# Two hundred and eight groups of softmax work in an engine loop of eight pairs a turn, with four logit banks and two message banks

## The chip, the cores and the metric

The kernel runs on one core of a Trainium2 chip. The metric is the device time of one execution in microseconds, as the median of the runs shown. The engines of the core are TensorE (PE; its weight loads are listed apart, as PEld), VectorE (DVE), ScalarE (ACT), GpSimd (POOL) and SyncE (SP), which here only starts transfers.

## The reference

Four graph layers run one after the other over a graph of 3125 nodes with 16 features and 100,000 edges sorted by destination. The change is in the second layer, a softmax over the incoming edges of each node, for each of 16 x 16 channels:

```python
w_m = (efeat @ W_msg + b_msg).reshape(E, in_f, -1)
w_a = (efeat @ W_attn + b_attn).reshape(E, in_f, -1)
h_src = feat[src][:, :, None]
e1 = w_m * h_src
e2 = w_a * h_src
seg_max = jax.ops.segment_max(e2, dst, num_segments=N)
ex = jnp.exp(e2 - seg_max[dst])
denom = jax.ops.segment_sum(ex, dst, num_segments=N)
attn = ex / denom[dst]
ft = jax.ops.segment_sum(e1 * attn, dst, num_segments=N)
return ft.sum(axis=1)
```

Around it stand a gated layer (`L0`), four graph convolutions (`L2`) and a sheaf layer (`L3`), each behind a layer norm and added to `x`.

## The kernel before

The program is a row of stages, each with its own stream of instructions per engine and a barrier behind it. The first stages sort the edges by blocks of 128 destination nodes (`NB` = 25 blocks) into 832 tiles (`NT`) of 128 slots, 416 pairs of tiles that never straddle two blocks, and 208 groups (`HT`) of four tiles (`HB`). Then come the middle stage (names `mid_`, written out on all engines), the update of the gated layer, the segment maximum (`segment_max`, names `mx_`, an engine loop on all engines, with gathers of node rows by GpSimd, L1236), `split_top` (the maxima as three bf16 parts, `m.top3`), and the stage that is changed, `soft_sums` (names `sm_`). Behind it come `attend`, a bucket table and the adjacency, the convolutions, the sheaf stage (names `sh_`, again a loop with gathers) and the end.

`soft_sums` is written out in full, with no loop on any engine. For a pair `r` of tiles:

- TensorE, `network(r)`: two bf16 matmuls into the logit bank `net_a` (L1564) and two into the message bank `net_m` (L1565), from the loaded edge features and the weights; one signal, `net_s`. There are three banks of each (`sets`), and the function waits for `both_s`, so for `weigh` of pair `r - 3`.
- VectorE, `enter(r)`: multiplies both by the features of the source nodes (`m.held`), L1506 (`arg_s`) and L1507 (`mess_s`).
- TensorE, `top(r)`: six bf16 matmuls (L1578) take the block's maxima from the logits, spread by the one-hot `hot_t`; `tops_s`.
- ScalarE: the exponential, L1549, into the first half of `both`; `exp_s`.
- VectorE, `weigh(r)`: messages times exponentials, L1512, into the second half; `both_s`.
- TensorE, `spread(r)`: two fp32 matmuls (L1591, recorded as four, with four weight loads) sum `both` over the slots of each node by the one-hot `hot`; `sums_s`.
- VectorE, `add(r)`: L1523, adds that to the block's part of `m.acc`; `kept`.

VectorE also makes the one-hots of each group, `hot_t` (L1495) and `hot` (L1223), and clears `m.acc` first (L1525). The order of the work is written out by hand. In step `r` TensorE does `network(r+3)`, `top(r+2)`, `spread(r+1)`, and VectorE `far_hot`, `enter(r+2)`, `weigh(r+1)`, `add(r)`, `spread_hot`. The block numbers are read into registers for eight pairs at a time (`blocks_of`). SP loads for each group the destination row (`low`, L1471) and the features (`feat`, L1472) into two halves, when `net_s` and `hot_t_s` say that the older ones are used.

GpSimd does other work meanwhile: once `rec2` and `row2` are loaded (L1474, L1475, behind the first two groups' loads on SP's queue), it scatters the records of the 832 tiles into a second order in DRAM (`slots2`), by 832 written-out indirect transfers (L1481) with no wait between them, and waits for all of them at the end.

Of the kernel before, what the change touches and what calls it, by code (L numbers as in the profile page):

```python
# [5 lines left out]
ALU = mybir.AluOpType  # L6
# [3 lines left out]
I32 = mybir.dt.int32  # L10
BF16 = mybir.dt.bfloat16
# [1431 lines left out]

def soft_sums(nc, m):

    turns, sets = NT // 2, 3
    with ExitStack() as ctx:
# [5 lines left out]
        net_a, net_m = ([ps(f"{n}{k}", [P, 2, 256]) for k in range(sets)] for n in ("net_a", "net_m"))  # L1453
        sums = [ps(f"sums{k}", [P, 512]) for k in range(2)]
        loaded = [sem("loaded0"), sem("loaded1")]
        names = ("hot_t_s", "hot_s", "net_s", "arg_s", "mess_s", "tops_s", "exp_s", "both_s", "sums_s", "kept", "cleared",
                 "ordered", "order_in")
        (hot_t_s, hot_s, net_s, arg_s, mess_s, tops_s, exp_s, both_s, sums_s, kept, cleared, ordered,
# [3 lines left out]
        @block.sync  # L1462
        def _(sp):
            low_rows = m.low_row.rearrange("(c n) -> c n", n=512)
            feats = m.feat_t.rearrange("k (c n) -> k c n", n=512)
            for n in range(HT):
                h = n % 2
                if n >= 2:
                    sp.wait_ge(net_s, 2 * n - 2)
                    sp.wait_ge(hot_t_s, n - 1)  # L1470
                sp.dma_start(low[:, h], low_rows[n:n + 1].to_broadcast([P, 512])).then_inc(loaded[h], 16)  # L1471
                sp.dma_start(feat[:, h], feats[:, n, :]).then_inc(loaded[h], 16)  # L1472
                if n == 1:
                    sp.dma_start(rec2[:, :, :], m.rec2_dram).then_inc(order_in, 16)  # L1474
                    sp.dma_start(row2[:, :], m.row2_dram).then_inc(order_in, 16)  # L1475
# [13 lines left out]
        def _(dve):  # L1489
            def far_hot(n):  # L1490
                h = n % 2
                dve.wait_ge(loaded[h], (n // 2 + 1) * 32)
                if n >= 2:
                    dve.wait_ge(tops_s, 2 * n - 2)
                nc.vector.tensor_scalar(hot_t[:, h], low[:, h], m.iota_col[:, 0:1], None, ALU.is_equal).then_inc(hot_t_s, 1)  # L1495

            def spread_hot(n):
                if n >= 2:
                    dve.wait_ge(sums_s, 2 * n - 2)
                one_hot(nc, m, LO, n, hot[:, n % 2]).then_inc(hot_s, 1)  # L1500

            def enter(r):
                k = r % sets
                src = m.held[:, 2 * r:2 * r + 2, :][:, :, :, None].to_broadcast([P, 2, D, D])
                dve.wait_ge(net_s, r + 1)
                nc.vector.tensor_tensor(four(net_a[k][:, :, :]), four(net_a[k][:, :, :]), src, ALU.mult).then_inc(arg_s, 1)  # L1506
                nc.vector.tensor_tensor(four(net_m[k][:, :, :]), four(net_m[k][:, :, :]), src, ALU.mult).then_inc(mess_s, 1)  # L1507

            def weigh(r):
                dve.wait_ge(exp_s, r + 1)  # L1510
                dve.wait_ge(mess_s, r + 1)
                nc.vector.tensor_tensor(both[:, r % 2, :, 1, :], net_m[r % sets][:, :, :], both[:, r % 2, :, 0, :], ALU.mult).then_inc(both_s, 1)  # L1512

            values = []

            def add(r):
                if r % 8 == 0:
                    values[:] = blocks_of(nc, m, mybir.EngineType.DVE, r, 8)
                row = m.acc[:, bass.ds(values[r % 8], 1), :].rearrange("q o c -> q (o c)")
                dve.wait_ge(sums_s, r + 1)  # L1520
                if r:
                    dve.wait_ge(kept, r)
                nc.vector.tensor_tensor(row, row, sums[r % 2][:, :], ALU.add).then_inc(kept, 1)  # L1523
# [715 lines left out]
```

## Time and profile before

| | us |
|---|---|
| runs | 10386.8 and 10391.05 |
| median | 10388.92 |
| profiled execution, span | 10386.0 |
| TensorE busy | 6161.5 (59%) |
| VectorE busy | 6112.8 (59%) |
| GpSimd busy | 4395.4 (42%) |
| ScalarE busy | 1635.9 (16%) |

The span runs from the first to the last instruction of one profiled execution; no time of its own is listed for what lies around it, and it is 0.8 us below the faster of the two runs. Busy shares are means over all the stages, which have different limits, so they say little of the one stage that is changed; the profile has to be cut by stage.

### The profile page before, as it was taken

To read this page: it belongs to the slowest core of one execution; us is meant where nothing else is said; L and a number is where in the kernel's file an instruction comes from. 1 tells how busy PE (TensorE), PEld (TensorE's weight loads), DVE (VectorE), ACT (ScalarE), POOL (GpSimd) and SP (SyncE) were. 2 spreads that over 40 slices of the span, in tenths; PEclk is the share of its full clock that TensorE was granted. 3 is DMA by queue.
4 is the path that set the end of the run, shared out by engine and by line. 5 is a ranking of instruction groups with operands and counts; after the bars stand their busy time and mean duration, and the time that the engine had idled before them with its cause. 6 is when DMAs were issued, how large, how long until landed. Compare 5 with 4: busy or idle time off the path is not lost. (4 is left out here: it accounts for less than half of the span.)

```text
span 10386.0 us, 121636 instructions
## 1 busy us (share of the span) xinstructions
PE 6161.5 (59%) x33600; PEld 4039.5 (39%) x33601; DVE 6112.8 (59%) x12781; ACT 1635.9 (16%) x2872; POOL 4395.4 (42%) x4142
## 2 busy tenths in 40 slices
PE   4433333144456777761111499984469967777799
PEld 2333332034455444440000255543434345555555
DVE  6666663143346777772000399999950056666798
ACT  0111110000012444330000022213400011222100
POOL 0577775456653666656777400000000055565300
PEclk9999997555557898885555699998999955555599
DMA  2222223111112222230000011112235611111000
GB/s 79 46 54 52 52 53 78 32 43 32 34 40 58 64 66 66 62 62 12 4 4 5 16 43 43 43 34 76 105 156 230 253 24 25 25 25 25 15 0 1
DMA packets 491139, 554.08 MB, mean 53 GB/s; under 512 B 259701, under 2 KB 390093, under 8 KB 477394
## 3 DMA queue, kind: packets, MB, share of 16 engines
q1 hardware_dynamic: 347558, 485.94, 14.3%
q0 software_dynamic: 132160, 43.97, 4.7%
q10 hardware_dynamic: 11232, 21.73, 0.8%
q8 instruction: 109, 1.79, 0.1%
q14 instruction: 80, 0.66, 0.0%
HBM read 454.32 MB, written 95.99 MB: 53 GB/s over the span
## 5 line engine op out<-in xcount | busy, mean ns | idle before, releaser
L1236 POOL DMA_INDIRECT sh_ring<-node,sh_idx x832 | 853.4, 1026 | 1879.2 <-DVE sh_idx L1841 1648.7
L1236 POOL DMA_INDIRECT mx_ring<-node,mx_idx x832 | 890.0, 1070 | 710.7 <-DVE mx_idx L1310 466.0
L421 POOL DMA_INDIRECT slots<-rank_staged,rank_row_i x800 | 952.3, 1190 | 398.6 <-issue 227.7
L1591 PE MATMUL sm_sums<-sm_both,sm_hot 128*128 128x512 f32 x1664 | 842.8, 631 | 468.3 <-issue 468.0
L898 POOL DMA_INDIRECT mid_ring<-typed,mid_idx x832 | 834.6, 1003 | 512.6 <-issue 245.5
L1481 POOL DMA_INDIRECT slots<-sm_rec,sm_row x832 | 859.5, 1033 | 335.6 <-issue 280.4
L401 PE MATMUL rank_found<-rank_next_sb,rank_hot_hi_t 25*125 25x128 f32 x1600 | 407.3, 431 | 824.5 <-ACT rank_next_sb L386 787.0
L401 PEld LDWEIGHTS rank_found<-rank_next_sb,rank_hot_hi_t 25*125 25x125 f32 x1600 | 353.6, 321 | 874.5 <-DVE rank_hot_hi_t L340 843.1
L1578 PE MATMUL sm_net_a<-top,sm_hot_t 128*128 x2496 | 361.6, 283 | 514.2 <-issue 486.9
L1103 PE MATMUL mid_sums<-mid_ring,mid_hot_d 128*128 128x17 f32 x1664 | 392.2, 347 | 356.0 <-issue 325.1
L1512 DVE TENSOR_TENSOR sm_both<-sm_net_m,sm_both 128x512 f32<-128x512 f32 x416 | 300.5, 722 | 477.0 <-issue 445.4
L1591 PEld LDWEIGHTS sm_sums<-sm_both,sm_hot 128*128 128x128 f32 x1664 | 297.7, 199 | 707.8 <-issue 698.8
L2081 PE MATMUL srl_sums<-srl_outer,srl_hot_lo 128*128 128x400 f32 x1664 | 561.0, 500 | 7.4 <-DVE srl_outer L2063 7.4
L1549 ACT ACTIVATE sm_both<-sm_net_a 128x512 f32<-128x512 f32 x416 | 248.4, 597 | 2005.6 <-PE sm_net_a L1578 866.9
L1103 PEld LDWEIGHTS mid_sums<-mid_ring,mid_hot_d 128*128 128x128 f32 x1664 | 404.6, 310 | 358.6 <-issue 358.5
L1417 PE MATMUL mx_best<-mx_run_e,mx_hot 128*128 128x256 f32 x1664 | 474.1, 430 | 117.3 <-ACT mx_run_e L1367 60.1
L1663 PE MATMUL c_sums<-strips,g 128*16 128x512 f32 (+3 forms) x1400 | 537.7, 547 | 0.0
L1334 DVE TENSOR_TENSOR_SCAN mx_run<-mx_far,mx_run,mx_logit 128x512 f32<-128x512 f32 x414 | 509.2, 1271 | 21.5
L521 POOL IOTA bt_iota<- 25x1408 f32 x1 | 1.3, 1295 | 1183.8 <-ACTq L509 1183.8
L1981 PE MATMUL sh_hid_ps<-sh_ends_t,mlp 32*128 32x512 f32 x416 | 392.7, 1095 | 175.5 <-ACT sh_ends_t L1934 120.7
L1506 DVE TENSOR_TENSOR sm_net_a<-sm_net_a,held 128x512 f32<-128x512 f32 x416 | 305.1, 733 | 289.4 <-remote 269.7
L1523 DVE TENSOR_TENSOR acc<-acc,sm_sums 128x512 f32 x416 | 299.0, 719 | 295.2 <-remote 215.1
(393 smaller groups left out, 12803.8 us busy)
## 6 DMA issues: line engine op xcount, KB each, us to landing
strips<-near SPq DMA_DIRECT2D x100, 1600.0 KB, 9.1
mx_far<-far_row SPq DMA_DIRECT2D x208, 256.0 KB
rank_key_row<-key_rows SPq DMA_DIRECT2D x200, 244.1 KB
near<-adj_whole SPq DMA_DIRECT2D x175, 256.0 KB, 2.0
sm_low<-low_row SPq DMA_DIRECT2D x208, 128.0 KB
sh_low<-low_row SPq DMA_DIRECT2D x104, 256.0 KB
feat_t<-mid_out ACTq DMA_DIRECT2D x104, 204.0 KB
mx_feat<-feat_t SPq DMA_DIRECT2D x208, 102.0 KB
```

Source lines behind the costliest of these rows:

```text
L401: last = nc.tensor.matmul(found[h][:, j, :], hot_hi_t[:, h, j, :], next_sb[:, h, j * P:(j + 1) * P], start=True, stop=True, skip_group_che ...
L421: pool.indirect_dma_start(m.slots, bass.IndirectOffsetOnAxis(ap=row_i[:, h, j:j + 1], axis=0), staged[:, h, j, :], None).then_inc(sent[h], 16)
L898: pool.indirect_dma_start(ring[:, n % DEEP, j, 0:D], None, m.typed, bass.IndirectOffsetOnAxis(ap=idx[:, t:t + 1], axis=0)).then_inc(gather ...
L1103: nc.tensor.matmul(sums[:, bass.ds(blocks[j // 2] * K17, K17)], hot_d[:, h, j, :], ring[:, n % DEEP, j, 0:K17], start=False, stop=True, sk ...
L1236: pool.indirect_dma_start(ring[:, h, j, :], None, table, bass.IndirectOffsetOnAxis(ap=idx[:, h, j:j + 1], axis=0)).then_inc(part, 16)
L1334: last = nc.vector.tensor_tensor_scan(run[:, h, c, :], far[:, h, :], logit[:, c, :], before, ALU.add, ALU.max)
L1417: last = nc.tensor.matmul(best[:, k, :], hot[:, h, 2 * k + j, :], run_e[:, h, 2 * k + j, :], start=j == 0, stop=j == 1, skip_group_check=True)
L1481: pool.indirect_dma_start(m.slots2, bass.IndirectOffsetOnAxis(ap=row2[:, t:t + 1], axis=0), rec2[:, t, :], None).then_inc(ordered, 16)
L1591: last = nc.tensor.matmul(sums[r % 2][:, :], hot[:, h, 2 * (r % 2) + j, :], both[:, r % 2, j].rearrange("q a c -> q (a c)"), start=j == 0, ...
L1663: last = nc.tensor.matmul(sums[:, c:c + w], m.g[:, s, 0:width], m.strips[:, k % RING, c:c + w], start=False, stop=s == NB - 1, skip_group_ ...
L1981: nc.tensor.matmul(hid_ps[:, c:c + 512], m.mlp1[:, :], ends_t[:, c:c + 512], start=True, stop=True).then_inc(hp_s, 1)
L2081: last = nc.tensor.matmul(sums[:, 0:NB * D], hot_lo[:, h, j, :], outer[:, h, j, :], start=False, stop=True, skip_group_check=True)
```

## The change

The stage's work is put into an engine loop on SP, VectorE, ScalarE and TensorE. `octets` runs the first turn, then a loop over the 50 middle turns, then the last one; a turn is eight pairs, and there are 52. GpSimd's stream is left as it is. Inside a turn:

- `network` is parted into `logits`, with four banks, which waits for `exp_s` of pair `r - 4`, and `messages`, with two banks, which waits for `both_s` of pair `r - 2`. Each has its own signal (`net_a_s`, `net_m_s`). `logits` waits for the loads for every pair, not for every second.
- TensorE's order is `logits(r+3)`, `top(r+2)`, `messages(r+3)`, `spread(r+1)`. VectorE's is `far_hot`, `enter(r+2)`, `weigh(r+1)`, `message(r+2)`, `add(r)`, `spread_hot`.
- The targets of the waits and the addresses of `m.held`, of the loaded rows and of the block numbers are worked out from the loop's register. Block numbers are read at the start of each turn.
- SP starts the loads of `rec2` and `row2` first; its load of `low` waits for `hot_t_s` alone, and its load of `feat` for `net_m_s`.
- Two small tables of the later adjacency stage, `m.table` and `m.marks`, hold 16-bit instead of 32-bit integers.

Removed lines are those of the function above, and are left out here.

```diff
...
+def octets(eng, total, body):
+    body(0)
+    with eng.Fori(0, total - 2) as i:
+        body(i + 1)
+    body(total - 1)
 def soft_sums(nc, m):
...
+    pairs, sets = NT // 2, 4
+    turns = pairs // 8
     with ExitStack() as ctx:
         sb, ps, sem = makers(nc, ctx, "sm")
         feat, low = sb("feat", [KP, 2, 512], BF16), sb("low", [P, 2, 512], FP16)
         hot_t, hot = sb("hot_t", [P, 2, 512], BF16), sb("hot", [P, 2, HB, P])
         both = sb("both", [P, 2, 2, 2, 256])
         rec2, row2 = sb("rec2", [P, NT, 2]), sb("row2", [P, NT], I32)
...
+        net_a = [ps(f"net_a{k}", [P, 2, 256]) for k in range(sets)]
+        net_m, sums = ([ps(f"{n}{k}", [P, 2, 256]) for k in range(2)] for n in ("net_m", "sums"))
         loaded = [sem("loaded0"), sem("loaded1")]
...
+        names = ("hot_t_s", "hot_s", "net_a_s", "net_m_s", "arg_s", "mess_s", "tops_s", "exp_s", "both_s", "sums_s", "kept",
+                 "cleared", "ordered", "order_in")
+        (hot_t_s, hot_s, net_a_s, net_m_s, arg_s, mess_s, tops_s, exp_s, both_s, sums_s, kept, cleared, ordered,
          order_in) = map(sem, names)
         block = ctx.enter_context(nc.Block())
@@ -1463,16 +1473,18 @@
         def _(sp):
             low_rows = m.low_row.rearrange("(c n) -> c n", n=512)
             feats = m.feat_t.rearrange("k (c n) -> k c n", n=512)
...
+            sp.dma_start(rec2[:, :, :], m.rec2_dram).then_inc(order_in, 16)
+            sp.dma_start(row2[:, :], m.row2_dram).then_inc(order_in, 16)
+            def turn(q):
+                for j in range(4):
+                    n, h = 4 * q + j, j % 2
+                    wait(sp, hot_t_s, n - 1)
+                    sp.dma_start(low[:, h], low_rows[bass.ds(n, 1)].to_broadcast([P, 512])).then_inc(loaded[h], 16)
+                    wait(sp, net_m_s, 2 * n - 2)
+                    sp.dma_start(feat[:, h], feats[:, bass.ds(n, 1), :].rearrange("k o n -> k (o n)")).then_inc(loaded[h], 16)
+            octets(sp, turns, turn)
         @block.gpsimd
         def _(pool):
@@ -1487,124 +1499,150 @@
         @block.vector
         def _(dve):
...
+            def far_hot(q, j):
+                n, h = 4 * q + j, j % 2
+                dve.wait_ge(loaded[h], (2 * q + j // 2 + 1) * 32)
+                wait(dve, tops_s, 2 * n - 2)
                 nc.vector.tensor_scalar(hot_t[:, h], low[:, h], m.iota_col[:, 0:1], None, ALU.is_equal).then_inc(hot_t_s, 1)
...
+            def spread_hot(q, j):
+                n = 4 * q + j
+                wait(dve, sums_s, 2 * n - 2)
+                one_hot(nc, m, LO, n, hot[:, j % 2]).then_inc(hot_s, 1)
+            def sources(r):
+                return m.held[:, bass.ds(2 * r, 2), :][:, :, :, None].to_broadcast([P, 2, D, D])
+            def enter(q, j):
+                r, net = 8 * q + j, four(net_a[j % sets][:, :, :])
+                dve.wait_ge(net_a_s, r + 1)
+                nc.vector.tensor_tensor(net, net, sources(r), ALU.mult).then_inc(arg_s, 1)
+            def message(q, j):
+                r, net = 8 * q + j, four(net_m[j % 2][:, :, :])
+                dve.wait_ge(net_m_s, r + 1)
+                nc.vector.tensor_tensor(net, net, sources(r), ALU.mult).then_inc(mess_s, 1)
+            def weigh(q, j):
+                r, h = 8 * q + j, j % 2
                 dve.wait_ge(exp_s, r + 1)
                 dve.wait_ge(mess_s, r + 1)
...
+                nc.vector.tensor_tensor(both[:, h, :, 1, :], net_m[h][:, :, :], both[:, h, :, 0, :], ALU.mult).then_inc(both_s, 1)
+            def add(q, j, where):
+                r = 8 * q + j
+                row = m.acc[:, bass.ds(where, 1), :].rearrange("q o c -> q (o c)")
                 dve.wait_ge(sums_s, r + 1)
...
+                wait(dve, kept, r)
+                nc.vector.tensor_tensor(row, row, sums[j % 2][:, :, :].rearrange("q a c -> q (a c)"), ALU.add).then_inc(kept, 1)
+            def turn(q):
+                blocks = blocks_of(nc, m, mybir.EngineType.DVE, 8 * q, 8)
+                for j in range(8):
+                    r = 8 * q + j
+                    ahead = inside(r + 2, pairs)
+                    if j % 2 == 0 and ahead:
+                        far_hot(q, j // 2 + 1)
+                    if ahead:
+                        enter(q, j + 2)
+                    if inside(r + 1, pairs):
+                        weigh(q, j + 1)
+                    if ahead:
+                        message(q, j + 2)
+                    add(q, j, blocks[j])
+                    if j % 2 == 0 and ahead:
+                        spread_hot(q, j // 2 + 1)
             nc.vector.memset(m.acc[:, :, :], 0.0).then_inc(cleared, 1)
             dve.wait_ge(cleared, 1)
...
+            far_hot(0, 0)
+            spread_hot(0, 0)
+            enter(0, 0)
+            message(0, 0)
+            enter(0, 1)
+            weigh(0, 0)
+            message(0, 1)
+            octets(dve, turns, turn)
         @block.scalar
         def _(act):
...
+            def turn(q):
+                for j in range(8):
+                    r = 8 * q + j
+                    act.wait_ge(tops_s, r + 1)
+                    wait(act, sums_s, r - 1)
+                    nc.scalar.activation(both[:, j % 2, :, 0, :], net_a[j % sets][:, :, :], ACT.Exp).then_inc(exp_s, 1)
+            octets(act, turns, turn)
         @block.tensor
         def _(pe):
...
+            def pair_feat(j, t):
+                c = (2 * (j % 2) + t) * P
+                return feat[:, j // 2 % 2, c:c + P]
+            def logits(q, j):
+                r = 8 * q + j
+                pe.wait_ge(loaded[j // 2 % 2], (2 * q + j // 4 + 1) * 32)
+                wait(pe, exp_s, r - sets + 1)
+                for t in range(2):
+                    last = nc.tensor.matmul(net_a[j % sets][:, t, :], pair_feat(j, t), m.w6[:, 256:512], start=t == 0, stop=False,
+                                            skip_group_check=True)
+                last.then_inc(net_a_s, 1)
+            def messages(q, j):
+                wait(pe, both_s, 8 * q + j - 1)
+                for t in range(2):
+                    last = nc.tensor.matmul(net_m[j % 2][:, t, :], pair_feat(j, t), m.w6[:, 0:256], start=True, stop=True,
+                                            skip_group_check=True)
+                last.then_inc(net_m_s, 1)
+            def top(q, j, where):
+                r, h = 8 * q + j, j // 2 % 2
+                pe.wait_ge(hot_t_s, 4 * q + j // 2 + 1)
                 pe.wait_ge(arg_s, r + 1)
...
+                for t in range(2):
+                    c = (2 * (j % 2) + t) * P
                     for part in range(3):
...
+                        last = nc.tensor.matmul(net_a[j % sets][:, t, :], hot_t[:, h, c:c + P],
+                                                m.top3[:, bass.ds(where, 1), part, :].rearrange("q o c -> q (o c)"),
                                                 start=False, stop=part == 2, skip_group_check=True)
                 last.then_inc(tops_s, 1)
...
+            def spread(q, j):
+                r, h = 8 * q + j, j // 2 % 2
+                pe.wait_ge(hot_s, 4 * q + j // 2 + 1)
                 pe.wait_ge(both_s, r + 1)
...
+                wait(pe, kept, r - 1)
+                for t in range(2):
+                    last = nc.tensor.matmul(sums[j % 2][:, :, :].rearrange("q a c -> q (a c)"), hot[:, h, 2 * (j % 2) + t, :],
+                                            both[:, j % 2, t].rearrange("q a c -> q (a c)"), start=t == 0, stop=t == 1)
                 last.then_inc(sums_s, 1)
...
+            def turn(q):
+                last = isinstance(q, int) and q == turns - 1
+                blocks = blocks_of(nc, m, mybir.EngineType.PE, 8 * q + 2, 6 if last else 8)
+                for j in range(8):
+                    r = 8 * q + j
+                    if inside(r + 3, pairs):
+                        logits(q, j + 3)
+                    if inside(r + 2, pairs):
+                        top(q, j + 2, blocks[j])
+                    if inside(r + 3, pairs):
+                        messages(q, j + 3)
+                    if inside(r + 1, pairs):
+                        spread(q, j + 1)
+            first = blocks_of(nc, m, mybir.EngineType.PE, 0, 2)
+            for j in range(3):
+                logits(0, j)
+            messages(0, 0)
+            messages(0, 1)
+            top(0, 0, first[0])
+            top(0, 1, first[1])
+            messages(0, 2)
+            spread(0, 0)
+            octets(pe, turns, turn)
 def attend(nc, m):
@@ -2188,7 +2226,7 @@
         renew_semaphores(nc)
         with ExitStack() as scope:
             rb = on(scope)
...
+            m.table, m.marks = rb("table", [1, NT2, 2], U16), rb("marks", [1, NB, 8], U16)
             bucket_table(nc, m)
             adjacency(nc, m)
```

## Rows read from the trace of the kernel before

**Rows 1.** The windows view, the two halves of the softmax stage.

```profile
core 0: us, PE busy (x) PEld busy (x) DVE busy (x) ACT busy (x) POOL busy (x), PEclk, DMA share, GB/s
4740.00:5856.00 1116.00, 169.97 (x400) 71.66 (x400) 89.22 (x143) 17.31 (x29) 841.08 (x814) 0.52 0.03 4
5880.00:6960.00 1080.00, 1078.51 (x5330) 630.05 (x5331) 1076.40 (x1906) 228.02 (x382) 0.00 (x0) 1.00 0.16 42
```

**Rows 2.** The source view, the scatters and the summing matmuls, first to last.

```profile
L1481 POOL DMA_INDIRECT slots<-sm_rec,sm_row x832: 963/969/1911, 4717.6 to 5856.6; - x167
...
L1591 PE MATMUL sm_sums<-sm_both,sm_hot x1664: 592/592/1222, 4726.6 to 6966.3; 128*128 128x512 f32 x185
```

**Rows 3.** The groups of instructions, first half (4740 to 5856).

```profile
L1591 PE MATMUL sm_sums<-sm_both,sm_hot 128*128 128x512 f32 x116 | 108.9, 1093 | 452.3 <-issue 452.3
```

**Rows 4.** The groups of instructions, second half (5880 to 6960).

```profile
L1591 PE MATMUL sm_sums<-sm_both,sm_hot 128*128 128x512 f32 x1524 | 722.5, 596 | 15.2 <-issue 15.2
```

**Rows 5.** The timeline of one pair in the first half.

```profile
5040.78 0.70 DVE L1506 TENSOR_TENSOR sm_net_a<-sm_net_a,held 128x512 f32<-128x512 f32 x1 [10.17 <-remote]
...
5057.57 0.60 ACT L1549 ACTIVATE sm_both<-sm_net_a 128x512 f32<-128x512 f32 x1 [38.63 <-issue]
...
5063.16 0.42 PE L1565 MATMUL sm_net_m<-w,sm_feat 102*128 102x256 bf16 x1
...
5068.88 0.69 DVE L1523 TENSOR_TENSOR acc<-acc,sm_sums 128x512 f32 x1 [9.99 <-remote]
...
5080.00 0.70 DVE L1506 TENSOR_TENSOR sm_net_a<-sm_net_a,held 128x512 f32<-128x512 f32 x1 [9.83 <-remote]
```

**Rows 6.** The timeline in the segment maximum.

```profile
3666.20 0.94 POOL L1236 DMA_INDIRECT mx_ring<-node,mx_idx  x1 [1.39 <-DVE mx_idx L1310]
...
3667.64 0.38 PE L1382 MATMUL mx_src_ps<-ident_bf,mx_ring 128*48 128x128 bf16 x4 [0.32 <-issue]
3668.05 0.58 ACT L1352 COPY mx_src_t<-mx_src_ps 48x512 bf16<-48x512 bf16 x1 [1.98 <-PE mx_src_ps L1382]
...
3673.61 0.38 PE L1382 MATMUL mx_src_ps<-ident_bf,mx_ring 128*48 128x128 bf16 x4 [0.53 <-DMA mx_ring<-node,mx_idx]
...
3675.62 0.94 POOL L1236 DMA_INDIRECT mx_ring<-node,mx_idx  x1 [0.30 <-issue]
3677.89 0.58 ACT L1352 COPY mx_src_t<-mx_src_ps 48x512 bf16<-48x512 bf16 x1 [5.99 <-DMA rec_feat<-in_edge_attr]
...
3679.29 0.17 DVE L1310 CAST mx_idx<-fields 128x4 int32 x1 [0.35 <-issue]
```

**Rows 7.** The timeline in the middle stage.

```profile
2519.73 0.29 PEld L1103 LDWEIGHTS mid_sums<-mid_ring,mid_hot_d 128*128 128x128 f32 x1 [1.81 <-issue]
2520.43 0.19 PE L1103 MATMUL mid_sums<-mid_ring,mid_hot_d 128*128 128x17 f32 x1 [1.22 <-issue]
...
2521.89 0.18 DVE L1016 COPY mid_ring<-fields 128x8 f32<-128x8 f32 x1 [23.35 <-remote]
...
2522.60 1.40 POOL L898 DMA_INDIRECT mid_ring<-typed,mid_idx  x1 [4.88 <-remote]
```

**Rows 8.** The timeline at the start of the softmax stage.

```profile
4709.12 0.34 SPq L1471 DMA_DIRECT2D sm_low<-low_row  x1
...
4711.10 10.72 DVE L1525 MEMSET acc<- 128x12800 f32 x1 [3.02 <-issue]
```

**Rows 9.** The groups of instructions, whole span, a loop of the adjacency.

```profile
L637 DVE TENSOR_TENSOR adj_heavy<-adj_now,adj_near 128x1024 bf16<-128x1024 bf16 x528 | 332.5, 685 | 0.0
```

**Rows 10.** The DMA view, 5900 to 6900, fetched instructions.

```profile
q8 instruction: 46, 0.75, 0.3%
```

**Rows 11.** The DMA view, 8600 to 9600, in the looped sheaf stage.

```profile
q0 software_dynamic: 18528, 5.97, 8.0%
q1 hardware_dynamic: 10368, 18.88, 5.9%
...
sh_low<-low_row SPq DMA_DIRECT2D x72, 256.0 KB
```

More of the change, by code:

```diff
@@ L10 @@
 I32 = mybir.dt.int32
+U16 = mybir.dt.uint16
 BF16 = mybir.dt.bfloat16
@@ L1525, in _ @@
             nc.vector.memset(m.acc[:, :, :], 0.0).then_inc(cleared, 1)
             dve.wait_ge(cleared, 1)
-            far_hot(0)
-            spread_hot(0)
-            enter(0)
-            enter(1)
-            weigh(0)
-            for r in range(turns):
-                if r % 2 == 0 and r + 2 < turns:
-                    far_hot(r // 2 + 1)
-                if r + 2 < turns:
-                    enter(r + 2)
-                if r + 1 < turns:
-                    weigh(r + 1)
-                add(r)
-                if r % 2 == 0 and r + 2 < turns:
-                    spread_hot(r // 2 + 1)
+            far_hot(0, 0)
@@ L1551, in _ @@
+            octets(act, turns, turn)
         @block.tensor
         def _(pe):
-            values = []
-            def network(r):
-                n, k, h = r // 2, r % sets, r // 2 % 2
-                if r % 2 == 0:
-                    pe.wait_ge(loaded[h], (n // 2 + 1) * 32)
-                if r >= sets:
-                    pe.wait_ge(both_s, r - sets + 1)
-                for j in range(2):
-                    c = (2 * (r % 2) + j) * P
-                    f = feat[:, h, c:c + P]
-                    nc.tensor.matmul(net_a[k][:, j, :], f, m.w6[:, 256:512], start=j == 0, stop=False, skip_group_check=True)
-                    last = nc.tensor.matmul(net_m[k][:, j, :], f, m.w6[:, 0:256], start=True, stop=True, skip_group_check=True)
-                last.then_inc(net_s, 1)
@@ L1581, in top @@
                 last.then_inc(tops_s, 1)
-            def spread(r):
-                n, h = r // 2, r // 2 % 2
-                if r % 2 == 0:
-                    pe.wait_ge(hot_s, n + 1)
+            def spread(q, j):
+                r, h = 8 * q + j, j // 2 % 2
+                pe.wait_ge(hot_s, 4 * q + j // 2 + 1)
                 pe.wait_ge(both_s, r + 1)
-                if r >= 2:
-                    pe.wait_ge(kept, r - 1)
-                for j in range(2):
-                    last = nc.tensor.matmul(sums[r % 2][:, :], hot[:, h, 2 * (r % 2) + j, :],
-                                            both[:, r % 2, j].rearrange("q a c -> q (a c)"), start=j == 0, stop=j == 1)
-                last.then_inc(sums_s, 1)
@@ L1595, in _ @@
-            network(0)
-            network(1)
-            network(2)
-            top(0)
-            top(1)
-            spread(0)
-            for r in range(turns):
-                if r + 3 < turns:
-                    network(r + 3)
-                if r + 2 < turns:
-                    top(r + 2)
-                if r + 1 < turns:
-                    spread(r + 1)
+                wait(pe, kept, r - 1)
+                for t in range(2):
+                    last = nc.tensor.matmul(sums[j % 2][:, :, :].rearrange("q a c -> q (a c)"), hot[:, h, 2 * (j % 2) + t, :],
+                                            both[:, j % 2, t].rearrange("q a c -> q (a c)"), start=t == 0, stop=t == 1)
```

57 lines of the change are left out of this document (removed).

## Prediction

> **What bounds the kernel now.** I read the windows view first, and cut the softmax stage at the end of GpSimd's work. The stage has two halves that have nothing in common [rows 1]. From 4740 to 5856 us TensorE is busy 170 of 1116 us, VectorE 89, ScalarE 17; only GpSimd works, 841 us. From 5880 to 6960 us GpSimd does nothing, and TensorE (1078.5) and VectorE (1076.4) are busy in all of the 1080 us. The source view tells what parts them: the 832 scatters of L1481 run from 4717.6 to 5856.6, (5856.6 - 4717.6) / 831 = 1.37 us each, while the matmuls of L1591 are spread over the whole stage [rows 2].
>
> Four records of L1591 make one pair of tiles (1664 for 416). The line groups show 116 in the first half, 29 pairs, 1116 / 29 = 38.5 us each [rows 3], and 1524 in the second, 381 pairs, 1080 / 381 = 2.83 us each [rows 4]. So half of the stage is lost somewhere: at the second rate the 29 pairs take 82 us.
>
> Where they are lost is to be read in the timeline of one pair [rows 5]. VectorE's multiplication (L1506) runs at 5040.78, ScalarE's exponential behind TensorE's `top` starts at 5057.57, VectorE's `add` at 5068.88, its next multiplication at 5080.00: 39.2 us a pair. The last matmul of `network` (L1565) is drawn at 5063.16 and takes 0.42 us, yet VectorE, which waits for just it, starts 16.4 us later, released by nothing on its own engine ("remote"). VectorE and ScalarE need their usual 0.6 to 0.7 us for an instruction as soon as they are released. What is late is each signal of TensorE, in TensorE's order. The delays go with the array instructions (weight loads and matmuls) behind each signal: `top` has 12 and comes 16.8 us after 5040.78, `spread` has 8 and comes 11.3 us later, `network` has 8 and comes 11.1 us later: 39.2 / 28 = 1.40 us for each, about one for each scatter of GpSimd. I call this the drag.
>
> The drag is not only here. In the segment maximum, where TensorE and GpSimd already run engine loops, ScalarE's copy starts right at the end of L1382 once (3667.64 + 0.38, copy at 3668.05), and 5.6 us later starts 3.9 us behind it (3673.61 + 0.38, copy at 3677.89), and then GpSimd has just sent a run of gathers without a pause [rows 6]. In the middle stage, which is written out on all engines, a weight load and a matmul are drawn 0.70 us apart, and all is well again when GpSimd has paused for 4.88 us [rows 7]. So the drag needs an unpaused stream of GpSimd's transfers, and appears beside looped and unlooped TensorE alike.
>
> **The change part by part.** *GpSimd* keeps its 832 scatters, unlooped, without a wait. The stream lasts its 1139 us as before [rows 2]. Its two loads are now first on SP's queue instead of behind four others, which brings it forward by four issues at 0.34 us, 1.4 us [rows 8]; TensorE's first operands come later by as much, but VectorE's memset of the sums, 4711.10 to 4721.82, is still running then, so that costs nothing [rows 8]. If that cover were gone it would be 1 us.
>
> *Banks.* Four logit banks instead of three let `logits` run a pair further ahead of the exponential; two message banks instead of three tie `messages(r+3)` to `weigh(r+1)`. In the first half this gives nothing: what bounds there is the number of array instructions, still 28 a pair (`logits` 4, `messages` 4, `top` 12, `spread` 8). In the second half both engines are full already; `messages(r+3)` waits for the same `both_s` that `spread(r+1)`, right behind it in TensorE's order, waits for anyway, and `top(r+2)` in front of it takes the time that VectorE needs for `weigh(r+1)`. VectorE needs those messages a whole pair (2.83 us) later. Taken at 0, and below nothing is excluded, since no idle time is there to be won [rows 1].
>
> *SP.* The load of features now waits for the messages, half a pair later than the joint signal before, the loads run three pairs (8.5 us) ahead of their use; nothing.
>
> *Narrower tables* (32 to 16 bits) are written and read behind the stage. The adjacency's VectorE products L637 are back to back, 528 with 0.0 us idle before them [rows 9], and what reads the tables there is ScalarE and TensorE. Nothing.
>
> *The loop itself.* Semaphore targets and the addresses of `held` and of the loaded rows come out of registers now, on all four engines. In the first half the engines idle, and this hides. In the second half it is paid where a queue runs dry. From below the trace bounds it at 0.0 us: L637 stands in an engine loop with register waits and shows no gap [rows 9]. From above: a VectorE instruction in the looped segment maximum shows 0.35 us of "issue" before it [rows 6]; for each of 5.5 VectorE operations a pair that is 1.9 us, 387 pairs (416 - 29) x 1.9 = 745 us. I take the nearer row to be L637's, full and back to back like this half, and grant one gap of 0.35 us for each turn of eight pairs, when the loop goes back and the eight block numbers are read: 381 / 8 x 0.35 = 17 us.
>
> *A rule that speaks against the loop.* Instruction packets are seen in the second half: 46 on queue 8, 0.3% of 16 x 1000 us, 48 us in all or 1.04 us each [rows 10]. No engine waited for them: both were full [rows 1]. The Trainium skill, "Runtime: NRT & Kernel Launch", section "Instruction fetch mechanics", says that a taken branch to a target outside the two pages at hand must fetch it before going on, and that kernels prefer full unrolling for it. What this case shows against it here is the looped sheaf stage: 1000 us with 72 loads of `sh_low`, two a turn, 36 turns, and its list of queues has GpSimd's and the data's only, none of instructions [rows 11]. If nevertheless each turn fetched once or twice and waited for it, 52 x 1.04 = 54 us, or 108.
>
> Sum: span 10386.0 + 17 = 10403. The span is 2.9 us under the median of the two runs, 10388.9; so 10406, I say **10405 us**.
>
> **The rivals.**
>
> *The drag stays, as forecast.* For it: GpSimd's stream is beside every late signal [rows 5 to 7] and isn't touched; the looped segment maximum has the drag as well. Even if the loop made it worse, TensorE could lose at most the 29 pairs, 82 us, as the stream ends at its own time.
>
> *A milder drag.* The straight-line stages have the worst of it: 1.40 and 0.70 us for an instruction. Were it 0.70, as in rows 7, the first half held 1116 / 19.6 = 57 pairs instead of 29: 28 x 2.83 = 79 us less, 10326. The looped segment maximum sets the other end: the two copies of rows 6 are 9.84 us apart, with TensorE's 24 matmuls and 24 weight loads of a turn between them (by the code 2 and 2 of L1391 and L1396, 8 and 8 of L1409 and L1417, 4 of L1382), 0.205 us each. At that, a pair takes 5.7 us, 194 fit, 165 x 2.83 = 467 us less: 9938. Against: its run of gathers had lasted only 8 us there, and here the stream goes on for 1139.
>
> *The drag is gone.* That would be so if it came from TensorE's long straight line of instructions, and the stream only brought it out. Both badly hit stages have such a line, which speaks for it. Against: ScalarE and VectorE have one here too and are not late once released, and the 3.9 us in the looped stage. The stage would then take 416 x 2.83 + 16 = 1193 us instead of 2255 (from the memset at 4711.1 to the last of L1591 at 6966.3 [rows 2, 8]): 10405 - 1062 = 9343. The stream's 1139 us would no longer be the longest.
>
> *The loop's registers cost more than the full engines have to spare (slower).* The place is the second half: TensorE has eight waits on a register's value a pair, VectorE seven or eight and two register addresses for `held`. For each microsecond a pair 387 us follow. At the 0.35 us of rows 6 before half the VectorE operations it is 1.0 us, 10790; at one such gap and a half, 0.5 us, 10595. It passes 2% from 208 / 387 = 0.54 us a pair. Against: rows 9, and that a sequencer runs ahead while its engine is full.
>
> *Fetching at each turn* (the page's rule): 54 to 108 us, so 10460 to 10515, not slower by 2%. Against: the list of queues of rows 11.
>
> **How the numbers follow.** Drag as before 0.55; milder at about 0.7 us 0.08; milder at about 0.2 us 0.09; gone 0.13; registers 0.10, of which 0.08 above 2%; fetching 0.05. Two per cent, 208 us, is about what a measurement of this kernel tells from no change. Faster by over 2%: 0.09 + 0.13 = 0.22, with the milder cases between 0.24. Slower: 0.08, with a worse stall of unknown kind 0.09. Within 2%: 0.67. The likeliest case's own range is 10370 to 10490 (registers 0 to 0.2 us a pair, or one stall at each turn). The range that holds 8 in 10 needs 0.55 + 0.08 + 0.05 + the small half of the registers' case 0.04 = 0.72, and so the milder drag down to 9938 as well, 0.81: 9930 to 10590.
>
> **What would show it.** Right: four records of L1591 a pair still number about 116 between 4740 us and GpSimd's last scatter; ScalarE's exponential still starts 16 to 17 us behind VectorE's multiplication; after the stream 2.83 to 2.9 us a pair, with VectorE's idle time under 5%. The drag gone or milder: more than 200 such records beside the scatters, and a stage that ends near 5900 or 6500. Registers: "issue" time before the VectorE lines in the second half, and over 3.3 us a pair. Fetching: instruction packets at every turn, and a gap in all engines every 22.7 us. What would make me wrong is chiefly that I take the drag for GpSimd's doing alone; nothing in one trace has TensorE looped beside a stream as long as this one.

## The result and the profile after

The changed kernel takes 10838.8 us (10838.3 and 10839.2) against 10388.9: ratio 1.0434 (95%: 1.0414 to 1.0454), 450 us slower. The softmax stage behaves as forecast. The time goes where the prediction said "Nothing": into the adjacency, through the 16-bit tables.

The windows view of the kernel after, the two halves of the softmax stage and 300 us of the adjacency:

```profile
4740.00:5856.00 1116.00, 166.11 (x408) 69.71 (x407) 92.97 (x144) 17.33 (x29) 827.01 (x815) 0.53 0.03 4
5880.00:6960.00 1080.00, 1070.29 (x5241) 612.65 (x5242) 1063.23 (x1876) 224.56 (x376) 0.00 (x0) 1.00 0.15 41
...
7400.00:7700.00 300.00, 134.41 (x1230) 121.14 (x1231) 169.75 (x311) 80.17 (x138) 0.00 (x0) 0.56 0.16 61
```

The first two rows stand beside [rows 1]: again an idle half and a full half. For the third, a stretch of the adjacency in the kernel before:

```profile
7080.00:7400.00 320.00, 161.16 (x2296) 136.52 (x2294) 311.46 (x581) 143.75 (x251) 0.00 (x0) 0.97 0.27 106
```

The groups of instructions of the two halves (answering [rows 3] and [rows 4]):

```profile
L1618 PE MATMUL sm_sums<-sm_both,sm_hot 128*128 128x512 f32 x118 | 103.2, 1027 | 0.0
...
L1618 PE MATMUL sm_sums<-sm_both,sm_hot 128*128 128x512 f32 x1499 | 706.6, 593 | 0.0
```

118 records where there were 116, and 1499 for 1524: 2.88 us a pair for 2.83. The source view, first and last:

```profile
L1618 PE MATMUL sm_sums<-sm_both,sm_hot x1664: 591/592/1062, 4733.5 to 6984.1; 128*128 128x512 f32 x185
```

4733.5 to 6984.1 is 2250.6 us, where [rows 2] had 2239.7: the stage is 11 us longer, and starts 7 us later, although nothing ahead of it was changed.

The third window shows what is new. In the adjacency VectorE, busy in 311 of 320 us before, is now busy in 170 of 300, TensorE in 134 and ScalarE in 80, at a granted clock of 0.56 (0.97 before): no engine is full. The source view of what writes and reads `adj_sums`, before and after. Columns: count, shortest, median and longest duration in ns, first and last start. Before:

```profile
L668 PEldq TENSOR_LOAD <-table x176: 1102/1106/1527, 7078.9 to 7656.6; - x176
L675 PE MATMUL adj_sums<-adj_heavy,adj_hot x4224: 217/218/308, 7095.4 to 7660.0; 128*128 128x128 bf16 x192
```

After:

```profile
L669 PEldq TENSOR_LOAD <-table x176: 3783/4074/4893, 7096.8 to 8105.4; - x176
L676 PE MATMUL adj_sums<-adj_heavy,adj_hot x4224: 217/308/312, 7112.9 to 8111.9; 128*128 128x128 bf16 x192
```

TENSOR_LOAD is TensorE's sequencer fetching 16 registers of `m.table` for a turn of eight tiles. It took 1.11 us and takes 4.07. The turns, from first to last load over 175, went from 3.30 to 5.76 us: 2.46 x 176 = 433 us. With the 7 us ahead of the softmax stage and the 11 in it that is 451, the whole difference. The timeline of one turn, after:

```profile
7303.93 2.48 PEld L676 LDWEIGHTS adj_sums<-adj_heavy,adj_hot 128*128 128x128 bf16 x24 [3.15 <-issue]
7303.94 2.74 PE L676 MATMUL adj_sums<-adj_heavy,adj_hot 128*128 128x128 bf16 x24 [2.89 <-issue]
...
7306.83 0.17 DVE L632 COPY adj_now<-adj_fld 128x40 bf16 x1 [2.32 <-PE adj_sums L676]
```

and before, where VectorE has no idle time and TensorE waits for it:

```profile
7314.06 0.17 DVE L631 COPY adj_now<-adj_fld 128x40 bf16 x1
...
7314.27 1.55 PE L675 MATMUL adj_sums<-adj_heavy,adj_hot 128*128 128x128 bf16 x24 [1.67 <-DVE adj_heavy L637]
```

VectorE now waits for TensorE (2.32 us), and TensorE for nothing on another engine ("issue"): its sequencer loads.

### The profile page after: what moved, and what is told of

It reads as the page before. It is cut to its first block and busy times, and to the rows that moved or that the text cites. A ratio compares the mean times of both kernels' runs of the same rounds, so it can differ in the third digit from the quotient of the medians.

```text
span 10836.5 us, 125200 instructions
## 1 busy us (share of the span) xinstructions
PE 6353.9 (59%) x33600; PEld 4194.9 (39%) x33601; DVE 6132.0 (57%) x12781; ACT 1638.3 (15%) x2872; POOL 4386.0 (40%) x4142
## 5 line engine op out<-in xcount | busy, mean ns | idle before, releaser
L676 PE MATMUL adj_sums<-adj_heavy,adj_hot 128*128 128x128 bf16 x4224 | 454.4, 296 | 547.0 <-issue 401.2
L676 PEld LDWEIGHTS adj_sums<-adj_heavy,adj_hot 128*128 128x128 bf16 x4224 | 409.0, 136 | 593.8 <-issue 593.8
L1607 PEld LDWEIGHTS sm_net_a<-top,sm_hot_t 128*128 128x128 bf16 x2496 | 243.9, 99 | 609.5 <-issue 572.2
```

The costliest lines, as they stand in the source:

```text
L676: last = nc.tensor.matmul(sums[:, bass.ds(at[2 * j], P)], hot[:, h, j // 2, :, j % 2], heavy[:, h, k, j // 2, :, j % 2], start=False, stop ...
L1607: last = nc.tensor.matmul(net_a[j % sets][:, t, :], hot_t[:, h, c:c + P], m.top3[:, bass.ds(where, 1), part, :].rearrange("q o c -> q (o c)"),
```

## The experiments

Theory A: the narrow tables alone cost the time, as each register load is slow and TensorE's sequencer has to wait for it. B: the loop spoils what comes behind it. C: it is ScalarE's table (`marks`) that holds up the others. D: the load matters little, but TensorE's clock falls in the longer pauses. The kernel before has no masks. Of the test kernels, those in which `table` or both tables have 32 bits carry a mask (`& 255`, `& 4095`) on the loaded values that they wait for. That is a second difference, and one run measures it on its own.

**Loop alone, tables alone.** The changed kernel with wide tables:

```diff
-m.table, m.marks = rb("table", [1, NT2, 2], U16), rb("marks", [1, NB, 8], U16)
+m.table, m.marks = rb("table", [1, NT2, 2], I32), rb("marks", [1, NB, 8], I32)
-                    pe.wait_ge(evac, at[2 * j + 1])
+                    pe.wait_ge(evac, at[2 * j + 1] & 255)
-                    act.wait_ge(done, until[k])
+                    act.wait_ge(done, until[k] & 4095)
```

> The changed kernel with its two tables back at 32 bits (the loaded wait values are masked, one register operation each). Theory A, that the narrow tables alone cost the time: the load of the table's 16 registers takes 1.1 us again instead of 4.07, the adjacency's matmuls end about 565 us after they start instead of 999, and the whole takes 10405 us, ratio to before 1.000 to 1.003 (softmax stage +11 us). Rival B, that the loop of the softmax stage spoils what comes behind it (the clock, the state of TensorE's sequencer): it stays near 10839 us, ratio 1.043.

Measured 10447.7 us, ratio 1.0063 (1.0046 to 1.008); the load is back at 1107 ns. B falls. A had said 10405, so 43 us are left to explain; they come below. The kernel before with the first edit turned round (I32 to U16) and nothing else:

> The kernel before, with nothing changed but the two tables at 16 bits. Theory A: the register loads take 4.07 us each, the adjacency is 434 us longer, 10389 + 434 = 10823 us, ratio 1.042. Rival B: 10389 us, ratio 1.000.

Measured 10822.2, ratio 1.0423 (1.0405 to 1.044), within 1 us of A's figure, the load 4063 ns. So nearly all of the 450 us comes with one line of the diff, and without the loop.

**Which table.** The kernel before with U16 for `marks` alone, TensorE's waits masked:

> The kernel before with only the marks, ScalarE's 25 loads of 8 registers, at 16 bits, and TensorE's table at 32 (its loaded wait values masked, 8 register operations of about 0.04 us a turn). Theory A puts the loss on TensorE's 176 loads of the table: 10389 to 10400 us, ratio 1.000 to 1.001, since ScalarE idles in the adjacency. Rival C, that ScalarE's later copies hold TensorE and VectorE: 25 loads of 8 registers at 0.19 us more for each register are 37 us, 10425 us, ratio 1.004.

Measured 10437.5, ratio 1.0054 (1.0037 to 1.0071). ScalarE's load goes from 549 to 2110 ns for 8 registers, and TensorE's stays at 1107. The 55 us looked like C's 37 and more. But the kernel with masks and both tables wide has them too:

> The kernel before, unlooped, 32-bit tables, with nothing changed but the register operation that masks each loaded wait value in the adjacency (8 a turn on TensorE, 7 for each of ScalarE's 25 loads). The adjacency's turn had 0.5 us to spare on TensorE and gets 8 operations of 0.04 to 0.1 us between its matmuls. If those explain what is left of the looped kernel with wide tables (+65 us), this one is about 50 us over the kernel before, and the loop itself costs some 10 us. If the loop costs the 65 us, this one is at the kernel before.

Measured 10437.4, ratio 1.0043 (1.0029 to 1.0058). So it is the masks, and C falls: the adjacency's turn is 3.57 us for 3.30 in both, (7729.8 - 7104.3) / 175 with wide marks and (7698.3 - 7074.5) / 175 with narrow ones. The expectation for the narrow marks had put the masks at 0 to 11 us. A mask is an operation of 32 ns, but it takes more of the sequencer's time than that. From the first to the last of the eight waits of a turn, TensorE's sequencer takes 0.83 us on average before and 1.49 with the masks: 0.66 us more, of which the turn had about 0.5 to spare. The load is 0.08 longer here on average, and together they give the 0.27.

**Width or packing.** 32-bit cells, each followed by an unused one:

```diff
-rb("table", [1, NT2, 2], I32)
+rb("table", [1, NT2, 2, 2], I32)
-m.table[0:1, bass.ds(n * BT, BT), :].rearrange("o t k -> o (t k)")
+m.table[0:1, bass.ds(n * BT, BT), :, 0].rearrange("o t k -> o (t k)")
```

> As the kernel with narrow marks only, but the table's 32-bit cells stand 8 bytes apart, with an unused cell between any two. If what makes the register load slow is that the cells are narrower than a register, it stays at 1.1 us and the total near 10390 us. If it is that two cells of 16 bits share four bytes, or the spacing in general, a spacing other than the packed one could cost as well: 4 us and near 10820 us.

Measured 10930.0 in one run, slower than the narrow tables: the masks come on top, and now nothing hides them. The source view:

```profile
L669 PEldq TENSOR_LOAD <-table x176: 3789/4096/4902, 7070.0 to 8195.6; - x176
```

4.10 us with full-width cells, and (8195.6 - 7070.0) / 175 = 6.43 us a turn. So width isn't what counts; from both of these forms a register takes 0.25 us.

Nor do packed 32-bit cells suffice for a fast load. The looped softmax stage shows it: TensorE reads the eight block numbers of a turn from packed 32-bit cells, but from cell 8q + 2 on, where the kernel before starts at a multiple of eight. After, 5880 to 6960 us:

```profile
L780 PEldq TENSOR_LOAD <-pair x47: 1930/1937/1937, 5885.6 to 6941.5; - x47
```

and before:

```profile
L779 PEldq TENSOR_LOAD <-pair x47: 587/590/593, 5901.4 to 6940.7; - x47
```

1.94 us for 0.59, again 0.24 us a register, while VectorE's load of the same numbers, which starts at 8q, stays at 0.60. The start is the difference that can be seen, but it wasn't tried by itself. And in the middle stage of the kernel before (3068 to 3140 us) loads of four packed cells, starting at multiples of four, take 1.10 us each, while the same line takes 0.33 us at many other turns; why isn't shown. So the 16-bit and the spaced cells are enough to make a load slow, and other things can do it too.

**Half the registers.** Narrow cells, but column and wait value in one:

```diff
+nc.vector.scalar_tensor_tensor(m.table[:, :], tmp_i[:, :], 256.0, slot_i[:, :], ALU.mult, ALU.add)
+pe.wait_ge(evac, at[j] & 255)
+... sums[:, bass.ds((at[j] >> 8) * P, P)] ...
```

> The kernel before with narrow tables, but column and wait value of a tile packed into one 16-bit cell, so that a turn of the adjacency loads 8 registers instead of 16 and parts them with a mask and a shift each. If the load costs 0.25 us for each narrow register one after the other, it takes 2.1 us instead of 4.07, a turn is 1.97 us shorter and some 0.4 us longer by the parting: 176 x 1.57 = 276 us less than the narrow kernel, so 158 us over the kernel before. If a narrow load has a fixed price, it stays 434 us over.

Measured 10655.9, ratio 1.0252 (1.0235 to 1.0269), 166 us less than with 16 narrow registers and not 276.

```profile
L670 PEldq TENSOR_LOAD <-table x176: 1917/2201/2919, 7117.2 to 7950.5; - x176
```

The load is 2.20 us as expected, 1.87 less, but the turn is (7950.5 - 7117.2) / 175 = 4.76 us, 1.00 less: the parting costs 0.87 us, not 0.4. The load's price goes about with the number of registers (0.28 us each for 8, 0.25 for 16); the parting I had sized too low.

**The clock.** Two fp32 matmuls of zeros at the end of each turn, with narrow tables (and one wait ahead of all turns, left out here):

```diff
+                for _ in range(2):
+                    nc.tensor.matmul(sums[:, 7 * 512:8 * 512], zeros[:, 0:P], zeros[:, :], start=False, stop=True,
+                                     skip_group_check=True)
```

> The kernel before with narrow tables (10822 us), and TensorE has two more fp32 matmuls of zeros into a bank that nobody reads at the end of each of the adjacency's 176 turns, which run while the sequencer loads registers. In the narrow kernel the granted clock in this stage is 0.56 instead of 0.97. If the load itself paces the turns (4.07 us and the issue of 24 matmuls, 5.6 us), a higher clock wins nothing: 10822 to 10900 us. If the lost clock paces them, the matmuls of a turn fall from 2.74 to 1.55 us and the turn by 1.2 us, 176 x 1.2 = 211 us less: 10610.

This ran on another chip, where the kernel before takes 8491.8 us (more on this below); measured 8929.8 in one run, 438 us over. Windows view, in the adjacency, and source view:

```profile
5800.00:6200.00 400.00, 273.20 (x1916) 169.39 (x1915) 223.42 (x411) 106.18 (x184) 0.00 (x0) 0.87 0.16 60
```

```profile
L669 PEldq TENSOR_LOAD <-table x176: 3783/4085/4856, 5491.3 to 6507.0; - x176
L676 PE MATMUL adj_sums<-adj_heavy,adj_hot x4224: 217/218/312, 5507.1 to 6512.4; 128*128 128x128 bf16 x192
```

The clock is up (0.87), the median matmul is back at 218 ns, and the turn still takes (6507.0 - 5491.3) / 175 = 5.80 us. D falls: TensorE's sequencer, with its load, sets the turn at either clock, and the low clock of the changed kernel costs nothing that can be seen.

**The slow half of the softmax stage.** The drag, TensorE's late signals, was as strong in the loop. First I took the stream out of the stage, into a block of its own ahead:

> The looped kernel with 32-bit tables (10448 us), and GpSimd's 832 scatters in a block of their own ahead of the softmax stage, so that nothing streams beside it. If the drag on TensorE's signals comes from the stream: the scatters take 1140 us alone, then 416 pairs at 2.83 us take 1195 us, together about 2345 us where the stage took 2255, so about 10530 us, and no pair takes longer than 3 us. If the stage's first 29 pairs are slow for another reason (loads, the clock, a cold start), they are slow again: about 11500 us.

9612.0 us in one run, but on the chip where the kernel before takes 8491.8, so 1120 us *more*, about the length of the stream that now runs alone; of the drag this says nothing. The unlooped, unpaused kernel of the clock experiment, on that chip too, tells why. Its groups of instructions from 4200 to 5360 us:

```profile
L1486 POOL DMA_INDIRECT slots<-sm_rec,sm_row x805 | 887.8, 1103 | 273.9 <-issue 273.9
L1596 PE MATMUL sm_sums<-sm_both,sm_hot 128*128 128x512 f32 x1647 | 778.5, 595 | 0.2 <-issue 0.2
```

412 pairs in 1160 us beside the same stream: this chip has no drag in this stage at all. So pauses of GpSimd, tried on the same chip, could only cost:

```diff
             for t in range(NT):
+                if t and t % 4 == 0:
+                    pool.wait_ge(ordered, 16 * t)
```

> The looped kernel with 32-bit tables (10448 us), GpSimd waiting after each four scatters until all so far have landed. If the drag needs an unpaused stream, as the prediction read it, there is none: the softmax stage is as long as the longer of 1195 us of VectorE's work and 208 x (4 x 1.27 + about 2 us of landing) = 1470 us, instead of 2255, and the total near 9665 us, ratio 0.93. If the drag depends on how many scatters are sent, and not on the pauses: 1470 us of them at 38.5 us a pair, then 378 pairs x 2.83 = 1070, so 2540, total near 10730, ratio 1.033.

> The same with a wait after each eight scatters. If the drag sets in only behind more than eight in a row: 104 x (8 x 1.27 + 2) = 1265 us, total near 9460, ratio 0.91. In the segment maximum it showed in part behind a run of eight, at about 0.2 us for an array instruction (5.7 us a pair): 1265 / 5.7 = 222 pairs, then 194 x 2.83 = 549, 1814 us, total near 10005, ratio 0.96.

Ratios 1.0303 (1.0286 to 1.0321) and 1.0093 (1.0077 to 1.011). The second kernel, once more, on a chip like the first:

> The looped kernel with wide tables and a wait after each eight scatters once more. The four kernels before this call ran on a chip where the kernel before takes 8492 us and the softmax stage shows no slow half, so nothing could be learned of the pauses. On a chip like the first (kernel before at 10389): 9460 to 10005 us, ratio 0.91 to 0.96, if an unpaused stream is what the drag needs; 1.03 if pauses don't help. On a chip like the second: 1.009 again.

There the kernel before takes 10388.9, and this one 9963.9, ratio 0.9602 (0.9575 to 0.9629), against a loop without pauses at 1.0066. Its groups from 4740 to 5950 us:

```profile
L1495 POOL DMA_INDIRECT slots<-sm_rec,sm_row x818 | 807.3, 987 | 403.8 <-issue 251.5 <-DMA slots<-sm_rec,sm_row 152.3
L1620 PE MATMUL sm_sums<-sm_both,sm_hot 128*128 128x512 f32 x902 | 545.3, 737 | 0.0
```

902 / 4 = 225.5 pairs in 1210 us, 5.4 us each, beside nearly as many scatters as passed 29 pairs at 38.5 us before. So the pauses between the scatters, not their number, decide. The 5.7 us a pair that was forecast from the segment maximum fits as a mean, and only as one: from one `add` to the next, the pairs take 2.9 us at the tenth percentile and 8.6 at the ninetieth. There is no steady 0.2 us for an array instruction. Of the kernels tried this is the best on such a chip, and it beats both kernels there.

**The loop's own cost.** Looped with wide tables again, beside the masked kernel without a loop:

> The looped kernel with wide tables and masked waits once more, on the same chip as the masked kernel without the loop: the loop's own cost is the difference of the two. Theory: 5 to 20 us, whichever chip it is. Rival: the loop hides its costs in the slow half of the softmax stage only on a chip where that half is slow, and costs more (0.1 us a pair and over, 40 us) where all 416 pairs run at full rate.

10465.8, ratio 1.0066 (1.0048 to 1.0085), 28 us over the masked one, with intervals that overlap. By the source views the stage, first to last of its summing matmuls, is 2252.5 us in place of 2239.3: 13 us, and the rest lies elsewhere. Four more, looped and straight, with a wait after each four scatters, and with GpSimd paced by the sums of the pair:

```diff
+                if t % 2 == 0 and t > 2:
+                    pool.wait_ge(sums_s, t // 2 - 1)
```

> The looped kernel with wide tables, GpSimd waiting for its transfers after each four scatters, on the kind of chip where the softmax stage has a slow half (a wait after each eight gave 9964 us there, ratio 0.960). The stream lasts 1411 us by the run on the other chip. If four in a row don't reach TensorE's signals at all, the stage is 1411 us plus its end and start, 840 us under the unpaused 2255: 10460 - 830 = 9630, ratio 0.927. If the drag only depends on the share of time in which transfers are in flight: 0.94 to 0.96.

> The kernel before, unlooped, with masked waits (10437 us) and the same wait after each four scatters. If the straight line of TensorE's instructions plays no part in the drag: as the looped one less about 25 us, 9605 us, ratio 0.925. If the loop helps TensorE beside the paused stream, this one is 100 us or more slower than the looped one.

> The looped kernel with wide tables; GpSimd waits before each two scatters for the sums of the pair that belongs to them, not for its own transfers. Where TensorE's signals are late, GpSimd sends less. If the drag recovers as soon as the stream pauses by itself, the two settle between 2.83 and 5.7 us a pair, 1200 to 1900 us for the stage, total 9400 to 10100. If it doesn't recover without transfers having landed first: at 38 us a pair there is no drag either, since GpSimd then sends only two scatters in 38 us, so the worst is about that of the pauses.

> The same pacing in the kernel before, unlooped, with masked waits. If the loop plays no part: within 30 us of the looped one, and faster than it by 10 to 25 us.

They ran where the kernel before takes 8473.2 us: 8729.2 and 8742.9 (ratios 1.0302 and 1.0317), 8525.7 and 8529.9 (1.0058 and 1.0063). Looped and straight can't be told apart by the whole. By the stage they can. The source view, looped and paced:

```profile
L1620 PE MATMUL sm_sums<-sm_both,sm_hot x1664: 591/592/595, 4178.9 to 5367.9; 128*128 128x512 f32 x185
```

Straight and paced:

```profile
L1593 PE MATMUL sm_sums<-sm_both,sm_hot x1664: 592/592/1191, 4177.2 to 5350.2; 128*128 128x512 f32 x185
```

1189.0 against 1173.0 us: 16 us for 52 turns, 0.3 us each, with all 416 pairs at full rate. TensorE's load of block numbers is 1.35 us longer in each of these turns (1.94 for 0.59); most of that hides, and whether the 0.3 us is what doesn't wasn't tried.

The two that might say whether shorter runs of scatters take the drag away fully:

> The looped kernel paced by the sums once more, since the last call again ran where the kernel before takes 8473 us and nothing is late. On a chip like the first: 9400 to 10100 us, ratio 0.905 to 0.97, as stated before; on one like the second 1.006 again.

> The looped kernel with a wait after each four scatters once more. On a chip like the first 9630 us, ratio 0.927, if four in a row leave TensorE's signals alone, 0.94 to 0.96 if what counts is the share of time with transfers in flight; on one like the second 1.030 again.

Both met a chip without drag again (8485.5 before; 1.0053 and 1.0298). What shorter runs of scatters would give on one that has it stays open. On a chip without it the paced kernel costs little more than its masks (43 and 53 us in the two tries; the masks alone cost 48 on the first).

## Why the prediction was wrong

- **The narrow tables, "Nothing".** This is the step that failed, and the whole of the miss. It named who reads the tables, TensorE and ScalarE, and then argued from VectorE's being full, [rows 9], as if an engine that isn't the bound had unlimited room. The row it needed was in the trace: 176 loads of 1.11 us on TensorE's sequencer. With the issue of 24 matmuls a turn took TensorE's sequencer about 2.8 of 3.3 us, so it had 0.5 us to spare, and the load was about 40% of its work. (The 2.8 is 1.11 + 1.69, the rest of a turn after, 5.76 - 4.07. From rows of before alone, the load of 1.11 and the 1.55 us of the 24 matmuls leave 0.64 to spare.) A load of another form shows nowhere in the trace of before, and should have had a bound: each microsecond beyond the 0.5 costs 176 us, and 2% is passed at a load of 1.11 + 0.5 + 1.18 = 2.8 us. It was 4.07: (2.97 - 0.5) x 176 = 434, which agrees by construction, and (2.97 - 0.64) x 176 = 410 by the rows of before, against 433 measured.
- **The drag stays, looped or not.** Right: 118 records for 116. ScalarE's exponential started at 5067.79 behind VectorE's multiplication at 5052.53, 15.3 us against 16.8, a little under the 16 to 17 that were named as the sign.
- **The loop costs 17 us, one gap of 0.35 a turn.** Right in size: 11 us in the stage after, 13 and 16 in the two pairs of kernels with and without it. That the gap is the loop going back isn't shown: the turn also has TensorE's slower load of block numbers, which the prediction didn't see.
- **The registers' rival, above 0.54 us a pair.** Fell: 2.88 for 2.83. The range held neither this result nor its cause; the sign came out on its side, for a reason that wasn't its own.
- **Fetching at each turn.** It fell too: 16 us are 0.3 us a turn, under one of the 1.04 us that a packet took [rows 10]. And the turns fetch nothing: the DMA view of the kernel after, 5900 to 6900 us, 44 turns, lists no instruction packet, where before had 46 on queue 8. The rule of the Trainium skill, "Runtime: NRT & Kernel Launch", section "Instruction fetch mechanics", isn't contradicted, as no run shows a turn that had to fetch; the whole kernel fetches less than before, 58 packets on queue 8 for 109.
- **A milder drag, or none, through the loop.** Fell on the chip of the prediction. Both prices have been seen nevertheless: 5.4 us a pair by pausing the stream, and none on other chips. "The straight line is the cause" is out: the looped kernel has the drag on the first chip, and the straight one has none on the others.
- **Banks, order, SP.** Consistent with 0: the stage's 11 to 16 us leave no room for more, but they weren't tried by themselves.

## What to carry to other kernels

A load of registers from memory is work of a sequencer and has a row like any other: give it a duration, a place in the turn and a slack before a change to its table is called free. Keep tables that sequencers read packed and 32 bits wide, read off the trace what each load really takes (one that started at cell 8q + 2 was slow as well), and pack values only if the parting is cheaper than the register. When a diff has a small edit far from its subject, cost it on the engine that reads it, not on the one that is full.

## What the runs showed of the hardware

- A load of 16 registers takes 1.11 us from packed 32-bit cells, 4.07 from packed 16-bit cells and 4.10 from 32-bit cells 8 bytes apart; 8 registers take 0.55 to 0.60 us packed, 2.1 to 2.2 narrow, and 1.94 from packed 32-bit cells that start at 8q + 2: 0.07 against 0.24 to 0.28 us a register. Loads of four packed cells took 0.33 us, and in some stretches 1.10. The Trainium skill, "Runtime: NRT & Kernel Launch", section "Instruction fetch mechanics", gives about 200 ns a register for the runtime's own loads from HBM, in bulk too; the narrow and the spaced loads of SBUF here come near it, the packed ones of 1.11 us take about a third of it.
- A masking operation of 32 ns before each wait, eight in a turn of 24 matmuls, lengthened the turn by 0.67 us where TensorE's sequencer was the limit (6.43 for 5.76), 0.08 us each, and by 0.27 where it had 0.5 us to spare (3.57 for 3.30).
- Chips differ by 22% on one program: the median of the kernel before was 10383 to 10389 us in three sets of runs and 8473 to 8492 in three others, with less than 0.3% between the runs of a set. Two of the slow sets are from one chip, with a fast set from another in between (the third isn't attributed to one); the fast ones are from three chips. The difference lies in stages where GpSimd streams, as the drag does. With the same straight softmax stage and unpaused stream (the two kernels with narrow tables), first to last summing matmul take 2239 us on one and 1172 on the other, the stages ahead another 537, and the sheaf stage, with GpSimd's gathers, 1459 for 1147. The convolutions, where GpSimd sends nothing, take 517 us on both (L1767 to the last write of `g`). Why a chip has it isn't shown. Ratios across such chips mean nothing; each run here is compared with the kernel before on its own chip.
